# Softmax sums in a fused attention kernel: three accumulating DMAs a group in place of two, and one pass of ones in place of two

## The reference

```
q = (query @ Wq)   -> 32 heads of 32
k = (key @ Wk), v = (value @ Wv)   -> 8 heads of 32, each used by 4 query heads
scores = einsum('bhqd,bhkd->bhqk', q, k) * scale
probs = softmax(scores, axis=-1)
out = einsum('bhqk,bhkd->bhqd', probs, v)
return out @ Wo
```

## Time and profile before

| what | value |
|---|---|
| time, median of 3 runs | 861.71 (860.48 to 863.15) |
| profiled execution: time / span | 861.71 / 859.9 |
| TensorE matmul busy | 823.1, 96% |
| VectorE (DVE) busy | 589.0, 68% |
| GpSimd (POOL) busy | 534.4, 62% |
| ScalarE (ACT) busy | 448.6, 52% |
| granted TensorE clock, mean | 0.994 |

### The profile page before, as it was taken

The page is one execution under the profiler, slowest core; times in us unless marked ns, Lnnn a source line. Parts: engine busy times, 40 slices in busy tenths (PEclk is TensorE's granted clock), DMA queues, the critical chain, the costliest instruction groups (busy, mean ns, idle before and its releaser), DMA issues.

```text
span 859.9 us, 13955 instructions
## 1 busy us (share of the span) xinstructions
PE 823.1 (96%) x4458; PEld 331.4 (39%) x4458; DVE 589.0 (68%) x850; ACT 448.6 (52%) x741; POOL 534.4 (62%) x235
## 2 busy tenths in 40 slices
PE   6879899899999999999999999999999989999998
PEld 5557554344444432222322222322222213444443
DVE  4887748988387667888888888888888500455622
ACT  4456445565422237777777777777777772111200
POOL 5545319966534328888889888889988886211200
PEclk9989999999999999999999999999999999999999
DMA  8999963426996313554564455455455334122341
GB/s 264 262 269 229 205 185 98 111 74 107 237 232 150 125 58 78 105 127 101 120 133 101 105 106 119 95 131 132 95 115 103 80 67 98 21 54 49 58 137 73
DMA packets 120821, 107.79 MB, mean 125 GB/s; under 512 B 85324, under 2 KB 105804, under 8 KB 116684
## 3 DMA queue, kind: packets, MB, share of 16 engines
q1 hardware_dynamic: 115120, 71.59, 32.3%
q0 software_dynamic: 4608, 33.56, 19.3%
q10 hardware_dynamic: 1052, 2.10, 0.9%
HBM read 41.55 MB, written 12.58 MB: 63 GB/s over the span
## 4 chain that ended last, share of the span: by engine, by line
PE 69%; issue 7%; POOL 6%; DMA 5%; DVE 5%; POOLq 3%; DVEq 2%; ACT 2%; ACTq 0%
PE sbank L1662 12%; PE sbank L1653 12%; PE mpair L1593 11%; PE sbank L1471 3%; PE sbank L1473 3%; PE sbank L1472 3%; POOLq L493 3%; POOL wraw L599 3%; PE sbank L1729 3%; PE sbank L1733 3%; PE sbank L1744 3%; PE sbank L1746 3%; PE sbank L1731 3%; PE sbank L1672 3%; DMA tail<-wraw 2%
## 5 line engine op out<-in xcount | busy, mean ns | idle before, releaser
L1333 DVE TENSOR_REDUCE mx<-mpair 128x1 f32<-128x1024 f32 x256 | 302.3, 1217 | 63.6 <-PE mpair L1593 62.7
L891 ACT ACTIVATE regC<-sbank 128x512 f32<-128x512 f32 x512 | 277.9, 594 | 106.8 <-PE sbank L1653 105.9
L1653 PE MATMUL sbank<-regD 98*128 98x512 f16 x512 | 178.8, 385 | 7.9 <-ACT regC L891 5.6
L599 POOL TENSOR_TENSOR wraw<-regC 128x2048 f32<-128x2048 f32 x32 | 148.3, 4635 | 31.5 <-DMA tail<-wraw 16.3
L1593 PE MATMUL mpair<-regD 96*128 96x512 f16 x512 | 156.5, 381 | 0.7
L1662 PE MATMUL sbank<-regC,regD 128*32 128x512 f32 x1024 | 137.0, 607 | 1.0 <-ACT regC L891 1.0
L1653 PEld LDWEIGHTS sbank<-regD 98*128 98x128 f16 x512 | 48.6, 97 | 187.0 <-ACT regC L891 146.5
L599 POOL TENSOR_TENSOR regD<-regC 128x2048 f32<-128x2048 f32 x16 | 76.6, 4789 | 16.6 <-ACT regC L891 16.6
L599 POOL TENSOR_TENSOR tail<-regC 128x2048 f32<-128x2048 f32 x16 | 77.1, 4821 | 0.0
L1593 PEld LDWEIGHTS mpair<-regD 96*128 96x128 f16 x512 | 47.7, 98 | 54.2 <-DVE mx L1333 13.6
L492 POOL TENSOR_SCALAR xT_lo<-xT_lo,sc 128x1024 f32<-128x1024 f32 x16 | 29.1, 1821 | 48.7 <-DVE X L1001 37.5
(11 more groups left out here) (183 smaller groups left out, 1278.5 us busy)
## 6 DMA issues: line engine op xcount, KB each, us to landing
regD<-wraw POOLq DMA_DIRECT2D x16, 1024.0 KB, 7.0
tail<-wraw POOLq DMA_DIRECT2D x16, 1024.0 KB, 7.0
xT_lo<-in_ctx SPq DMA_DIRECT2D x16, 512.0 KB, 4.5
wraw<-in_L_ffn_W_int SPq DMA_DIRECT2D x8, 512.0 KB, 5.0
X<-in_x SPq DMA_DIRECT2D x4, 1024.0 KB, 7.6
wraw<-in_L_xattn_Wq SPq DMA_DIRECT2D x8, 512.0 KB, 3.8
wraw<-in_L_xattn_Wo SPq DMA_DIRECT2D x8, 512.0 KB, 4.3
regD<-q_hi_scratch SPq DMA_DIRECT2D x32, 128.0 KB, 2.4
```

The costliest lines, as they stand in the source:

```text
L599: nc.gpsimd.tensor_tensor(p_sum[pr if pr < 3 else 1][:, :, :], probs[:, (2 * pr) % 4, :, :], probs[:, (2 * pr) % 4 + 1, :, :], ALU.add).th ...
L891: nc.scalar.activation(probs[:, kt % 4, h, :], bank[4 + h % 2], ACT.Exp, scale=SCALE).then_inc(s["exp_ok"], 1)
L1333: v.tensor_reduce(mx[m][:, bass.ds(n, 1)] if par is not None else mx[m][:, n:n + 1], slot[:, :, :], AX.XY, ALU.max).then_inc(s["mx_red"], 1)
L1653: pe.matmul(bank[4 + h % 2], kst[par][0:98, kt * P:(kt + 1) * P], qst[par][0:98, h * 512:(h + 1) * 512], start=True, stop=True).then_inc(s ...
```

## The change

GpSimd folds a third time. Buffers: `sum_a` (target of add 0) and `sum_c` (target of add 2) now exist twice and alternate by group; `sum_b` (`wraw`, target of adds 1 and 3) stays single. Fold 1 adds `sum_b` onto `sum_a`, fold 2 adds `sum_b` onto `sum_c`, and the new fold 3 adds `sum_c` onto `sum_a`; fold 3 of a group is issued by `last_fold` in the next group, after its add 0. TensorE then needs one pass of ones a group, `sums`, in key tile 7 of the next group. The second pair of buffers lies in X[:, 4:8, :]; that half of X is stored to HBM (`XS`, four stores of 512 KB) during the q projections and loaded back (one load of 2 MB) after `sums` of group 14. `invert` and `output` come a group later than before, the accumulator has two buffers, `o_low` runs on DVE, and TensorE's loop over groups is written out.

```
-        p_sum = [regD[...], wraw[...], tail[...]]
+        sum_a = [X[:, 4:6, :], regD[...]]
+        sum_b = wraw[...]
+        sum_c = [X[:, 6:8, :], tail[...]]
...
-        acc_sb = y[:, 0:512]
+        acc_sb = [y[:, 0:512], vtmp[:, 512:1024]]
...
+            def store_x(i):
+                sp.dma_start(XS[:, i, :], X[:, TB + i, :]).then_inc(s["x_st"], 16)
             w2_turn(2)
             store_q(0, 4, 0)
+            store_x(0)
...
             store_q(1, 0, 0)
+            store_x(1)
...
             store_q(1, 1, 1)
+            store_x(2)
             store_q(1, 2, 0)
+            store_x(3)
...
             step(G - 2, 2, 0, 1, more=False)
+            sp.wait_ge(s["x_st"], 16 * TB)
+            sp.wait_ge(s["ps_mm"], G - 1)
+            sp.dma_start(X[:, TB:T, :], XS[:, :, :]).then_inc(s["x_back"], 16)
...
+            def fold(dst, src, done):
                 pool.sem_inc(s["pool_gate"], 1)
+                nc.gpsimd.dma_start(dst[:, :, :], src[:, :, :], accum_op=ALU.add).then_inc(done, 16)
+
+            def last_fold(g, par):
+
+                pool.wait_ge(s["fold1"], 16 * g + 16)
+                pool.wait_ge(s["fold2"], 16 * g + 16)
+                fold(sum_a[par], sum_c[par], s["fold3"])
+
+            def att(g, par, n=2):
                 if n >= 2:
+                    pool.wait_ge(s["ps_mm"], g - 1)
+                add_probs(g, 0, sum_a[par])
                 if n >= 1:
+                    last_fold(g - 1, 1 - par)
+                add_probs(g, 1, sum_b)
+                if n >= 2:
+                    output(g - 2, par, isinstance(g, int) and g == 2)
+                pool.wait_ge(s["p_add"], NPAIR * g + 2)
+                fold(sum_a[par], sum_b, s["fold1"])
+                if n >= 2:
+                    pool.wait_ge(s["fold3"], 16 * g - 16)
+                add_probs(g, 2, sum_c[par])
+                pool.wait_ge(s["fold1"], 16 * g + 16)
+                add_probs(g, 3, sum_b)
+                pool.wait_ge(s["p_add"], NPAIR * g + 4)
+                fold(sum_c[par], sum_b, s["fold2"])
...
# ACT: acc_out into acc_sb[par]; o_high(g - 3) after key tile 0 (was o_high(g - 2) after key tile 4)
+                    if kt == 0 and n >= 3:
+                        o_high(g - 3)
...
# DVE
+            def att(g, cur, n_before=3, ahead=2):
                 for n in range(LEAD, ITEMS):
                     if ahead >= 1:
                         reduce_item(g + 1, nxt, n)
+                    if n == LEAD and n_before >= 2:
+                        invert(g - 2, 0)
+                    if n == LEAD + 3 and n_before >= 2:
+                        invert(g - 2, 1)
+                    if n == LEAD + 5 and n_before >= 3:
+                        o_low(g - 3)
...
# DVE after the last group
+            for n in range(2):
+                invert(G - 2, n)
+            o_low(G - 3)
             o_out(0)
+            o_low(G - 2)
             o_out(1)
...
             ln4(0, True)
+            o_low(G - 1)
+            dve.wait_ge(s["x_back"], 16)
...
# TensorE
+            def sums(g):
+                pe.wait_ge(s["fold3"], 16 * g + 16)
...
+                    m = pe.matmul(bank[7][HD * h:HD * h + HD, :], ones32[:, :], sum_a[g % 2][:, h, :],
+                                  start=True, stop=True)
...
-                    if kt in (0, 4) and not first:
-                        sum_half(g - 1, kt // 4, isinstance(g, int) and g == 1)
+                    if kt == KT - 1 and not first:
+                        sums(g - 1)
...
             stage_o(0, True)
-            sum_half(G - 1, 0)
             stage_o(1)
-            sum_half(G - 1, 1)
+            sums(G - 1)
```

More of the change, by code:

```diff
@@ L569, in _, with output @@
             nc.gpsimd.memset(kst[2][96:98, :], MROW).then_inc(s["kones2"], 1)
-            def output(g, first=False):
+            def output(g, par, first=False):
                 if not first:
@@ L579, in output @@
                     pool.wait_ge(w2_tr[1], 16 * NPAIR)
[L580 to L589, removed]
-                pool.wait_ge(s["exp_ok"], 32 * g + 8 * pr + 8)
[L593 to L600, removed]
@@ L602, in fold @@
-            def fold(g, half):
-                pool.wait_ge(s["p_add"], NPAIR * g + 2 * half + 2)
-                pool.sem_inc(s["pool_gate"], 1)
[L606 to L612, removed]
+                nc.gpsimd.tensor_tensor(o_sb, acc_sb[par], rsum_sb, ALU.mult).then_inc(s["o_ready"], 1)
@@ L623, in _ @@
             pool.wait_ge(q_st[1], 32 * KD)
[L624 to L630, removed]
+            pool.wait_ge(s["x_st"], 16 * TB)
+            att(0, 0, 0)
+            att(1, 1, 1)
+            att(2, 0)
+            att(3, 1)
+            with pool.Fori(2, G // 2) as i:
+                att(2 * i, 0)
+                att(2 * i + 1, 1)
+            last_fold(G - 1, 1)
+            output(G - 2, 0)
+            output(G - 1, 1)
             def y_low(t, first=False):
@@ L913, in att @@
                         if kt == 0 and h == 1 and n >= 1:
[L914 to L924, removed]
+                            acc_out(g - 1, 1 - par)
+                    if kt == 0 and n >= 3:
+                        o_high(g - 3)
+            for g in range(4):
+                att(g, g % 2, g)
+            with act.Fori(2, G // 2) as i:
+                att(2 * i, 0)
+                att(2 * i + 1, 1)
+            acc_out(G - 1, 1)
+            for g in range(G - 3, G):
+                o_high(g)
             def y_high(t, first=False):
@@ L1383, in att @@
                         reduce_item(g + 1, nxt, n)
-                if not first:
-                    invert(g - 1, 0)
+                    if n == LEAD and n_before >= 2:
[4 more added lines that the diff above has]
+                        o_low(g - 3)
                 for n in range(LEAD):
@@ L1390, in att @@
                         split_max(g + 1, cur, g // 3 + 1)
[L1391 to L1395, removed]
+            for g in range(4):
+                att(g, g % 3, g)
+            with dve.Fori(1, (G - 4) // 3) as i:
                 att(3 * i + 1, 1)
@@ L1619, in turn_max @@
                 pe.wait_ge(s["mx_red"], ITEMS * (g + 1))
-                if not (isinstance(g, int) and g < 2):
-                    pe.wait_ge(s["inv_ok"], g - 1)
+                if g >= 3:
+                    pe.wait_ge(s["inv_ok"], g - 2)
                 pe.transpose(bank[7][:, 0:P], mx[par][:, :], id32[:, :]).then_inc(s["mt_mm"], 1)
@@ L1664, in pv @@
                 m.then_inc(s["pv_mm"], 1)
-            def sum_half(g, half, first=False):
-                pe.wait_ge(s["p_fold"], 32 * g + 16 * half + 16)
-                if half == 0 and not first:
+            def sums(g):
+                pe.wait_ge(s["fold3"], 16 * g + 16)
+                pe.wait_ge(s["mt_cp"], min(g + 3, G))
+                if g > 0:
                     pe.wait_ge(s["inv_ok"], g)
                 for h in range(REP):
-                    m = pe.matmul(bank[7][HD * h:HD * h + HD, :], ones32[:, :], p_sum[2 * half][:, h, :],
-                                  start=(half == 0), stop=(half == 1))
+                    m = pe.matmul(bank[7][HD * h:HD * h + HD, :], ones32[:, :], sum_a[g % 2][:, h, :],
+                                  start=True, stop=True)
                 m.then_inc(s["ps_mm"], 1)
@@ L1712, in _ @@
             pe.wait_ge(s["kones2"], 1)
-            for g in range(1, 4):
+            for g in range(1, G - 2):
                 att(g, g % 3)
-            with pe.Fori(1, (G - 4) // 3) as i:
-                att(3 * i + 1, 1)
-                att(3 * i + 2, 2)
-                att(3 * i + 3, 0)
-            att(G - 3, 1)
             att(G - 2, 2, ahead=1)
```

38 lines of the change are left out of this document (22 added, 16 removed).

## The result

The changed kernel takes 890.69 us (median of 6 runs, 888.47 to 894.36). The kernel before, run in turn with it, takes 862.45. The ratio is 1.0331, with a 95% interval of 1.0314 to 1.0348: 3.3% slower. The profiled execution took 891.03, its span is 889.2, against 859.9 before.

A forecast was written before the change was run, and what follows sets the result against it. TensorE's loop and GpSimd's chain with its folds, equally long, were taken to hold each other. Steps of 25.6 + 14 x 26.3 + 4 against 379.2 gave +18.6; with +2.0, -0.9, +2, +0.5, +22.2 on 861.7: 884 us, range 868 to 901.

The forecast's parts named there:

- TensorE's loop: TensorE's time per attention group: one sum pass fewer saves 0.9, 25.04 to 24.3 us, hidden under GpSimd's 26.3.
- GpSimd's period: GpSimd's time from one second fold to the next: 26.3 us, bounds 25.6 to 27.1, against a chain of 25.08 before.
- Late landings: Folds landing late in GpSimd's loop, hitting two direct waits a group: total cost 4 us (3 to 6), 3.0 before.
- 3.0 becomes 4: Cost of late folds over the 15 steps between second folds, raised from 3.0 to 4 us (3 to 6).
- o_low on DVE: The output's low half on DVE takes about 0.6 and may queue behind GpSimd's add, some 2 hidden; charged 0.
- port: Rival: o_low on DVE waits a whole GpSimd add each group, TensorE's loop becomes 29.1; +61, 920 us; chance 6%.
- slack of 2.0: Time per group by which TensorE's loop may be delayed by o_low's wait on DVE and stay hidden: 2.0 us.
- Balance: Rival: fold landings of 6.6 bring GpSimd's loop to 24.7 (low bound) or 25.4; 859 to 864 us; chance 4%.
- X through HBM: Four 512 KB stores among q stores and Wo loads, charged 0.5 us (0 to 3); the 2 MB load back hidden.
- The start of stage_o: Behind the last attention group: stage_o's start on TensorE moves 2.0 us more than the last second fold.
- The tail: After stage_o starts: one sum pass fewer, -0.9 us; the remaining pass stalls 2 us (0 to 3.7) for the folds.
- +22.2: Whole kernel's forecast loss in us: +18.6 from the steps between second folds, with +2.0, -0.9, +2 and +0.5.

The follow-up runs named there:

- Experiment 2: Kernel before with one of two sum passes a group left out on TensorE, the other reading a buffer of ones: 866.98 us, ratio 1.0074.
- six_low_pool: Changed kernel with two source and two tail buffers, output ahead of the third fold, the output's low half on GpSimd: 861.53 us, ratio 0.9988 to the kernel before.
- olow_pool_after: Changed kernel with the output's low half back on GpSimd, in the wait before the third fold: 891.74 us, ratio 1.0326 to the kernel before.
- experiment 1: Kernel before with TensorE's loop over groups written out and nothing else: 864.48 us, ratio 1.0031.
- experiment 6: Changed kernel with groups 2 to 13 of TensorE as a loop of two rounds of six groups: 892.1 us, ratio 1.0353 to the kernel before.
- experiment 5: Changed kernel with the output's low half moved from DVE back to GpSimd, before the third fold: 891.74 us, ratio 1.0326 to the kernel before.
- experiment 3: Kernel before with only the trip of X's upper half added, four stores and one 2 MB load back: 861.41 us, ratio 0.9984.
- cover_after: Changed kernel with output moved back behind add 2, over the landing of fold 1: 885.69 us, ratio 1.0281 to the kernel before.
- one_pass_before: Kernel before with one sum pass a group left out on TensorE, the pass left reading a buffer of ones: 866.98 us, ratio 1.0074.
- sp_code_fit: Kernel before with 448 added SyncE waits a group, 288 behind the stage's loads and 160 behind the maxima: 865.9 us, ratio 1.0049.
- sp_code_before: Kernel before with 512 added SyncE waits a group in one place and SyncE's loop over groups written out: 886.44 us, ratio 1.025.

## Why the prediction was right, and where it was off

The direction, the range (884 forecast, 890.7 measured, inside 868 to 901) and the mechanism hold: the third fold puts two landings a group on GpSimd's direct path with less work over them.

- **TensorE's loop.** Its saving was to be real and worthless. Experiment 2 shows it worthless in the kernel before. In `six_low_pool`, where GpSimd hardly holds it, the period is 24.65 and TensorE busy 99.2%: 24.45 of work, against 24.3 taken.
- **GpSimd's period.** Forecast 26.3, undisturbed 26.35 to 26.43. Its parts, forecast and measured: second to third fold 7.36, 7.53; to add 1 0.61, 0.61; to output 4.49, 4.50; to fold 1 1.64, 1.21; to add 3 7.06, 7.42; to the next second fold 5.12, 5.11. Two errors of 0.4 cancel, which is luck: output to fold 1 costs what it costs before an add, but fold 1, which goes out right behind output with the third fold in flight, takes 1.18 to be issued instead of 0.88, its data ends 0.3 later, and add 3 starts that much later. Group 1 was forecast at 25.6; it took 26.40, of which 0.7 is a late fold.
- **Late landings: the term that was mis-sized.** Forecast 4 (3 to 6). Measured: 408.4 less 25.7 for group 1 and 14 x 26.35 leaves 13.8. That is 9.8 of the 10.6 by which the steps exceeded the forecast of 397.8. Second folds account for 10.3: seven of the first 15 have their third fold issued 8.1 to 9.8 after them instead of 7.5, and every one of the seven has an instruction fetch beside it, none of the other eight has. Four late fold 1s, each with a fetch beside it, make 3.3 more. The table splits the steps of both profiled executions; "excess" is the time over the undisturbed steps (25.08 before; 25.7 once and 26.35 after):
```
steps       before: q8 fetches, excess     changed: q8 fetches, excess
1 to 6      7, 1.3                          7, 4.7
7 to 11     0, 0.0                          5, 2.2
12 to 15    4, 1.7                          4, 6.9
```
Two things went wrong in the prediction. The smaller is "that its loop over groups is now written out changes no instruction of a group: 0". It changes no instruction, but q8 now has a packet every 21 to 34 us all through the stage, where the loop of before ran steps 7 to 11 without one: 2.2, as much as experiment 1 has for the same steps (2.0). The larger is the step from two direct waits to "3.0 becomes 4". The other ten steps have as many fetches as before, eleven, and cost 11.6 where they cost 3.0: before, the longest landings (the first folds of groups 4, 13 and 15, 8.1 to 8.7) had 7.46 of work over them, and now both folds of a group lie on direct waits. The split is read from one trace of each kernel, and which fold a fetch meets may differ; `olow_pool_after`, with as many fetches, has 12.8 in place of 13.8. No kernel with the change and a loop free of fetches was run, since the loop of six groups had as many in its second round as in its first (experiment 6).
- **o_low on DVE.** Taken at 0: right (experiment 5). It was blocked: its median is 2.10. Of its 16 records in the changed kernel, the 13 that start while one of GpSimd's adds runs all end 0.55 to 0.59 after that add, and take up to 3.62; the three that meet no add take 0.67 to 0.69. What the two engines contend for, no trace shows; "port" is only the rival's name. The price of 61 in that rival needed the wait to reach TensorE past its slack of 2.0, and it did not. The sum of that rival was also off by itself: 861.7 + 61 is 923, not 920.
- **The rival "Balance".** Its 859 to 864 does not follow from its periods. With the prediction's other terms, 24.7 gives some 857 and 25.4 some 870.
- **X through HBM.** Forecast 0.5, measured 0 (experiment 3).
- **The start of stage_o.** Forecast 2.0 more than the fold, measured 2.2, but I do not count it as confirmed. `cover_after` and `olow_pool_after` also have one sum pass and start it 6.50 and 7.28 before their last second fold, like the kernel before, while `one_pass_before` has 4.52. In the changed kernel TensorE's clock was granted at 0.72 on average from 733 to 745 us, a stretch in which TensorE was busy 7.3 of 12 us: it was granted at 0.50 from 736.5 to 743.3, behind 5.5 us of which TensorE was busy 2.8, and at 1.00 on both sides. `one_pass_before` has such a stretch too (0.86 from 706 to 718), while `cover_after` and `olow_pool_after` have 1.00 in the 12 us before their stage_o. That speaks for the clock and against the sum pass, but no run tests it, and it stays open.
- **The tail.** A stall of 2 was taken from the load back meeting the last second fold. That fold was late (its third fold went out 8.15 after it, with one instruction packet beside it), yet no stall came: stage_o had started only 4.74 before that fold, so the pass was that much later as well. It started at 767.11, 1.0 after the third fold's landing, so this was close. The load took 7.7, not 10.4, and landed at 751.6, 0.6 after the fold that it was to meet had been issued. The tail shortened by 1.2 against 0.9 for the one pass.

By the terms, measured less forecast: late landings +9.8, period and group 1 +0.8, stage_o +0.2, tail with its stall -2.3 (-1.2 for -0.9 + 2), stores -1.4 (-0.9 for +0.5). Together +7.1, which is what lies between +22.2 and +29.3.

## What to carry to other kernels

Work taken off an engine whose chain waits for transfers buys nothing when that work lay over a landing (890.69 without `o_low` on GpSimd, 891.74 with it); before a reorder, list for each wait what covers it, and after it again. A longer pipeline needs its extra buffers at the source of the transfer too: the same three folds cost 29 us with one source buffer, some 4 with two, and nothing with another target beside it. Where a chain waits directly for a DMA, late landings that were covered before come to count in full (the ten steps with eleven fetches cost 11.6 over the undisturbed ones where they cost 3.0), so give them a wide range in a forecast. Code size counts too: added code, on TensorE and on SyncE here, brought instruction fetches (q8 from 26 to 33, q14 from 15 to 42) that run among the data, and with a fetch of 16 KB beside it a fold's data ended at 7.1 to 7.6 on average, against 6.63 to 6.67 without a fetch.

## What was not expected of the hardware

- With an instruction packet beside it, the data of a 1 MB fold ends not at 6.63 but between 7.1 and 7.6 on average in the four kernels and at up to 8.3 (16 KB), at 6.8 on average and up to 7.1 (8 KB, sp_code_fit). The landing can be later still. In the changed kernel's second folds of 666.82 and 722.38 the data ended at 7.2 and 7.1, a fetch started at 7.2 and 7.0, the last closing packet started only at 8.1 and 7.9, and the landings are recorded at 9.2 and 9.1. In these two a fetch came between the data and the closing packets. That the landing follows the closing packet by 1.0 to 1.2 in these two, where it follows by 0.3 in undisturbed folds, is not explained.
- Fold 1 of the changed kernel, issued right behind output with the third fold in flight (6.3 after its issue), costs GpSimd 1.18 instead of 0.88 for the issue, and its data, with no fetch beside it, ends at 6.9 to 7.0 (once at 7.1) instead of 6.63. A fold in flight is not enough for that: in `cover_after` fold 1 goes out behind an add, 6.0 after the third fold and also with its data still moving, and costs 0.87. Nor is output ahead of it: in `six_low_pool` the third fold goes out behind output with none in flight and costs 0.86.
- 512 satisfied waits took SyncE 16.2 us in `sp_code_before`, 32 ns each: cheap one by one, but enough to make the loads behind them late.
